# A decoder layer's attention on one core: shorter branch softmax and gate mix on VectorE, one rope product and one shared power on GpSimd, the query scale folded into the keys

## The chip, the cores and the metric

The kernel runs as one program on one core of a Trainium2 chip. Its time is the device time in microseconds (us). A core has TensorE (PE, matrix products), VectorE (DVE), ScalarE (ACT), GpSimd (POOL) and SyncE (SP, which here issues the DMAs). Each engine works through its own list of instructions in order, and the engines wait for one another on semaphores.

## The reference, cut to what matters

The layer is attention, then cross-attention, then a mixture of experts. Only the attention changes. With 64 sequences of 64 tokens, width 128, 8 heads of 64 and one key and value head shared by all heads:

```python
q = rmsnorm(rope(h @ w_qc @ w_qup)); k = rmsnorm(rope(h @ w_k)); v = h @ w_v
scale = 1 / sqrt(64)
kc, vc = means of k and v over blocks of 32 tokens        # two blocks
pc = softmax([q @ kc * scale (masked), sink])             # compressed branch
ps = softmax(q @ k * scale (causal))                      # selected branch
pw = softmax([q @ k * scale (causal, window 64), sink])   # window branch
g = sigmoid(q @ w_gate + b_gate)                          # three gates
gates = g / max(sum(g), 1e-6)
out = (gates[0]*comp + gates[1]*sel + gates[2]*win) @ w_out_group @ w_out
x1 = layernorm(x + out)
```

With only 64 tokens the window covers everything, so the selected and the window branch share one set of exponentials `E` and differ only in their denominators: `Z` (the row's sum) and `Z` plus the sink's exponential.

## The kernel before, in words

The attention works on 32 tiles of 128 rows (two sequences each). Every engine runs through the same list of slots, 41 in all (32 tiles and a lag of 9). In a slot `s` each engine does, for several tiles at once, the stage that tile `s - lag` has reached: a tile has its projection in lag 0, rope and the sums of squares in lag 1 (`b`), the normalised key in lag 2 (`c`), transposes in lag 3 (`d`), scores and exponentials in lag 4 (`e`), the branch denominators and gate mix in lag 5 (`f`), the mixed weights `Pm` on GpSimd in lag 6 (`f` there), the products with `v` in lag 7 (`h`), the output product and the layer norm's statistics in lag 8 (`k`), and the layer norm's output `xo` in lag 9 (`l`). The order of the work inside a slot is written out by hand and is the order in which the engine executes it. Each engine unrolls the list completely, so nothing is reordered at run time.

What the change and the prediction touch, by engine, in the order of a slot:

- VectorE. `xo` of tile `l` (L461, a tensor-scalar operation whose two scalars are read from `mv` and `rs`), the row maxima out of PSUM (L465), the copy `s5` (L468), the negative scaled maximum `nb` (L473), the cosine product `ta` (L478), the block scores `un` (L482), the residual sum `r` (L488), the maximum over the blocks and the sink `mc` (L491, L500), the arguments of the small exponentials (L494, L507, L509), the rope sum (L504, which waits for GpSimd's `tb`), `bn_aggr` (L512), the block means of the keys (L518), the normalised key `kd` (L525), the variance plus epsilon `ve` (L530), the denominators `den` (L533 to L536), the sums of squares (L539), the reciprocals of all six denominators (L542), `ms` (L546), and then the gate mix (L549 to L565), which ends in `pa` and `pc`, the factors for GpSimd.
- GpSimd. The two halves of the sine product `tb` (L401, L403), the gate logits `gl` and arguments (L409, L412; they wait for `s5`), `Pm = E * pa` (L417) and `Pm += pc` (L422), then `rs = ve ** -0.5` (L427, waits for L530), `rinv = ms ** -0.5` for nine columns (L431, waits for L546), and `sc8 = rinv / 8` (L433).
- ScalarE. Eight exponentials with `scale=sc8` that also write the row sums `Z` (L350), the small exponentials `ex` (L356), and copies out of PSUM.

In VectorE's list the operation behind the last one of the gate mix (L565) is the next slot's L461:

```python
if l.live:
    l.wait(dve, ln_rstd)
    l.wait_ring(dve, stored, 16, back=2)
    V.tensor_scalar(xo[:, l.u2, :], r[:, l.u2, :], mv[:, l.u2, 0:1], rs[:, l.u2, 0:1], ...)
```

`ln_rstd` of tile `l` is counted up by L427 in the slot before, while L546 and L431 of that slot come later.

Of the kernel before, what the change touches and what calls it, by code (L numbers as in the profile page):

```python
# [93 lines left out]
def attention(nc, x, xT, table, table64, table32, v_dram, x1, tiles, later, disp):  # L94
# [8 lines left out]
    with ExitStack() as ctx:  # L103
# [22 lines left out]
        root = sb("root", [P, H])  # L126
# [8 lines left out]
        ms = sb("ms", [P, 2, 9])  # L135
        rinv = sb("rinv", [P, 4, 9])
# [32 lines left out]
        ve = sb("ve", [P, 2, 1])  # L169
        rs = sb("rs", [P, 2, 1])  # L170
# [153 lines left out]
        def _(act):  # L324
# [48 lines left out]
        def _(pool):  # L373
# [63 lines left out]
        def _(dve):  # L437
# [18 lines left out]
            def slot(at):  # L456
                b, c, d, e, f, k, l = (Tile(at, m) for m in (1, 2, 3, 4, 5, 8, 9))
                if l.live:
                    l.wait(dve, ln_rstd)
# [80 lines left out]
                if f.live:  # L540
                    n.upto(n_den)
                    n_rd = n.add(V.reciprocal(rd[:, :, :], den[:, :, :]))  # L542
                if b.live:
                    n.upto(n_ss)
                    b.free(dve, inv_rms, 2)
                    V.tensor_scalar(ms[:, b.u2, :], ss[:, :], 1.0 / D, 1e-6, ALU.mult, ALU.add).then_inc(mean_sq, 1)  # L546
                if f.live:
                    n.upto(n_rd)
                    n_gs = n.add(V.tensor_reduce(gs[:, :], rd[:, :, 3:6], AX.X, ALU.add))  # L549
                    n.add(V.tensor_tensor(a1[:, :], rd[:, :, 4], rd[:, :, 0], ALU.mult))  # L550
                    n_a2 = n.add(V.tensor_tensor(a2[:, :], rd[:, :, 5], rd[:, :, 1], ALU.mult))
                    n.upto(n_gs)
                    n_gs = n.add(V.tensor_scalar(gs[:, :], gs[:, :], 1e-6, None, ALU.max))
                    n.add(V.tensor_tensor(a3[:, :], rd[:, :, 2], rd[:, :, 3], ALU.mult))
                    n.upto(n_a2)
                    n.add(V.tensor_tensor(a1[:, :], a1[:, :], a2[:, :], ALU.add))
                    n.upto(n_gs)
                    n_rg = n.add(V.reciprocal(rg[:, :], gs[:, :]))
                if f.live:
                    n.upto(n_rg)  # L560
# [1021 lines left out]
```

## Time and profile before

| | |
|---|---|
| time, median of 3 runs | 776.14 us (773.79 to 778.46) |
| the profiled execution | 769.72 us |
| its span in the trace | 767.9 us |
| busy share of the span: PE, DVE, ACT, POOL | 74%, 71%, 58%, 60% |
| granted TensorE clock, mean | 0.882 |

The span is divided into 40 slices of 19.2 us; the attention fills slices 1 to 16 or so. In the rows below, times are from the start of the span. A row of a timeline has the start in us, the length in us, the engine, the line, the operation, the tensors written and read (`a_` stands for the attention, `x_` for the cross-attention, `m_` for the experts, `l_` for what the later stages share), and their shapes as partitions by columns. In square brackets stands how long the engine was idle before it and what it waited for. An operation's length includes time in which it has started and can't yet read or write; the next one's start can lie before its end.

### The profile page before, as it was taken

Reading aid. Unit: us, or ns where it says so; the run is one execution under the profiler, and the core shown is the slowest. Engines: PE = TensorE matmul, PEld = TensorE weight load, DVE = VectorE, ACT = ScalarE, POOL = GpSimd, SP = SyncE. Lnnn points to the kernel's source line nnn. Section 1 sums busy time; section 2 is a strip of 40 time slices with the busy share of each in tenths; the row PEclk is TensorE's granted clock in tenths of the full one; section 3 lists DMA queues with packets and bytes.
Section 4 is the critical chain, followed back from the end, with each engine's and each line's share of the span. In section 5 each row is a group of like instructions: output and inputs, shape, how many; then the busy total and the mean of one; then the engine's idle time right before and its main releaser. Section 6 shows DMA issues by size and latency. Waiting matters only on the chain. (4 is left out here: it accounts for less than half of the span.)

```text
span 767.9 us, 17025 instructions
## 1 busy us (share of the span) xinstructions
PE 566.4 (74%) x4772; PEld 430.1 (56%) x4772; DVE 547.6 (71%) x1867; ACT 444.8 (58%) x1362; POOL 462.4 (60%) x553
## 2 busy tenths in 40 slices
PE   4766777777767774798999898961004999999984
PEld 2445556555555563465767666651003988888832
DVE  2589999999999985277888878864013666677615
ACT  2588777777777762496787655530002565566506
POOL 4568777777777754465664577787550454555533
PEclk9999889999998889597999998985556999999998
DMA  6154444441111101210111111111111222222154
GB/s 232 35 180 159 168 167 144 165 136 33 34 42 35 37 25 30 76 29 22 43 39 37 33 54 32 33 50 46 38 42 38 55 72 65 67 68 69 41 211 125
DMA packets 65884, 57.78 MB, mean 75 GB/s; under 512 B 22133, under 2 KB 60154, under 8 KB 63490
## 3 DMA queue, kind: packets, MB, share of 16 engines
q1 hardware_dynamic: 60866, 46.14, 19.3%
q0 software_dynamic: 4352, 8.47, 3.3%
q10 hardware_dynamic: 576, 2.10, 0.7%
q8 instruction: 42, 0.69, 0.4%
q14 instruction: 48, 0.39, 0.2%
HBM read 25.86 MB, written 31.33 MB: 74 GB/s over the span
## 5 line engine op out<-in xcount | busy, mean ns | idle before, releaser
L1419 POOL DMA_INDIRECT y_dram<-m_y,m_blk x72 | 72.0, 1000 | 92.1 <-ACT m_y L1385 80.6
L350 ACT ACTIVATE a_E<-a_ps,a_nb,a_sc 128x64 f32<-128x64 f32 x256 | 99.5, 408 | 11.7 <-DVE a_nb L473 10.6
L986 POOL DMA_INDIRECT disp_dram<-l_R,x_pos x64 | 63.0, 984 | 24.8 <-issue 15.1
L431 POOL TENSOR_TENSOR a_rinv<-a_ms,a_halfneg 128x9 f32<-128x9 f32 x32 | 57.7, 1803 | 33.5 <-DVE a_ms L546 33.5
L309 PE MATMUL a_ps<-a_tab,a_xTt 128*128 128x512 f32 x64 | 38.7, 689 | 48.0 <-DVE a_r L488 41.7
L959 POOL TENSOR_TENSOR x_KB<-x_kT,l_table 128x1024 f32<-128x1024 f32 x32 | 61.9, 1935 | 6.9 <-ACT x_kT L907 6.6
L966 POOL TENSOR_TENSOR l_rs<-x_ve,l_halfneg 128x2 f32<-128x2 f32 x32 | 23.9, 748 | 55.6 <-DVE x_ve L1121 55.3
L1289 PE MATMUL m_ps<-l_table,m_blk 128*128 128x128 f32 x72 | 14.6, 285 | 55.9 <-DMA m_blk<-disp_dram 55.9
L1452 DVE TENSOR_SCALAR m_lin<-m_ps 128x512 f32<-128x512 f32 x36 | 24.9, 691 | 41.1 <-PE m_ps L1314 41.1
L350 ACT ACTIVATION_READ_ACCUMULATOR a_E<-a_ps,a_nb,a_sc 128x1 f32 x256 | 53.5, 209 | 0.0
L1367 ACT ACTIVATE m_th<-m_tTc 128x256 fp32r<-128x256 f32 x36 | 15.1, 418 | 61.9 <-DVE m_tTc L1441 61.9
L1075 DVE TENSOR_REDUCE x_mx<-x_ps 128x16 f32<-128x1024 f32 x32 | 39.0, 1218 | 6.6 <-PE x_ps L793 6.3
L317 PE MATMUL a_ps<-a_PT,a_VB 128*128 128x256 f32 x128 | 42.8, 468 | 0.0
L1377 ACT ACTIVATE m_sg<-m_ps 128x512 f32<-128x512 f32 x36 | 21.5, 597 | 35.0 <-PE m_ps L1314 35.0
L279 PE MATMUL a_ps<-a_KB,a_qT 128*64 128x138 f32 x512 | 41.1, 307 | 0.0
L266 PE MATMUL a_ps<-a_tab,a_Pm 128*128 128x128 f32 x128 | 26.4, 342 | 19.3 <-POOL a_Pm L422 19.3
L427 POOL TENSOR_TENSOR a_rs<-a_ve,a_halfneg 128x1 f32<-128x1 f32 x32 | 19.5, 610 | 34.2 <-DVE a_ve L530 34.2
L309 PEld LDWEIGHTS a_ps<-a_tab,a_xTt 128*128 128x128 f32 x64 | 10.4, 204 | 53.1 <-issue 48.1
L793 PE MATMUL x_ps<-x_KB,x_qT 64*64 64x512 f32 x256 | 36.9, 648 | 3.6 <-DVE x_sh L1097 2.8
L1289 PEld LDWEIGHTS m_ps<-l_table,m_blk 128*128 128x128 f32 x72 | 7.6, 145 | 56.4 <-DMA m_blk<-disp_dram 56.4
L892 ACT ACTIVATE x_PT<-x_ps 128x1024 f32<-128x1024 f32 x32 | 32.5, 1015 | 11.4 <-PE x_ps L782 11.3
L422 POOL TENSOR_TENSOR a_Pm<-a_Pm,a_pc 128x512 f32<-128x512 f32 x32 | 37.5, 1173 | 2.5
(234 smaller groups left out, 1990.8 us busy)
## 6 DMA issues: line engine op xcount, KB each, us to landing
disp_dram<-l_R SPq DMA_DIRECT2D x16, 1040.0 KB, 4.2
m_blk<-disp_dram SPq DMA_DIRECT2D x72, 65.0 KB, 1.9
a_xTt<-in_xT SPq DMA_DIRECT2D x32, 64.0 KB, 3.8
l_W1l<-in_w SPq DMA_DIRECT2D x1, 2048.0 KB
a_VB<-v_dram SPq DMA_DIRECT2D x128, 16.0 KB, 2.0
a_xt<-in_x SPq DMA_DIRECT2D x32, 64.0 KB, 2.0
x_dram<-a_xo SPq DMA_DIRECT2D x32, 64.0 KB, 1.7
x_xa<-x_dram SPq DMA_DIRECT2D x32, 64.0 KB, 1.9
```

What stands on the lines that cost most here:

```text
L279: last = nc.tensor.matmul(ps_S[D * q:D * q + D, c // 2, (c % 2) * 2 * W:(c % 2 + 1) * 2 * W], qT[:, e.u2, c, D * q:D * q + D], KB[:, e.u2, ...
L309: nc.tensor.matmul(flat[:, 0:512], xTt[:, a.u2, :], wqkv[:, 0:512], start=True, stop=True)
L317: last = nc.tensor.matmul(ps_mT.rearrange("p (c t) -> p c t", c=4)[:, :, D * q:D * q + D], VB[:, h.u4, q, :], PT[:, :, D * q:D * q + D], s ...
L350: last = nc.scalar.activation(E[:, e.u4, g, :], ps_Sh[:, g // 4, g % 4, 0:D], ACT.Exp, bias=nb[:, e.u2, g:g + 1], scale=sc8[:, e.u4, g:g + 1],
L422: G.tensor_tensor(Pv, Pv, pc[:, f.u2, :, :].rearrange("p h n -> p (h n)").unsqueeze(2) .to_broadcast([P, 2 * H, 32]), ALU.add).then_inc(mi ...
L431: G.tensor_tensor(rinv[:, b.u4, :], ms[:, b.u2, :], halfneg[:, 0:9], ALU.pow).then_inc(inv_rms, 1)
L793: last = nc.tensor.matmul(ps_S[T * q:T * q + T, 8 * g:8 * g + 8, :].rearrange("p h k -> p (h k)"), qT[s, d.t % 6, T * q:T * q + T], KB[s, ...
L892: nc.scalar.activation(PT[:, :, :], ps_PT, ACT.Copy).then_inc(PT_ready, 1)
L959: G.tensor_tensor(KB[:, c.t % 3, :, :, :], kT[:, c.u4, :].rearrange("p (b k) -> p b k", b=2).unsqueeze(2).to_broadcast([P, 2, 8, T]), hm[: ...
L986: G.indirect_dma_start(out=disp[:, :], out_offset=bass.IndirectOffsetOnAxis(ap=pos[:, B % 2, k_, t - base:t - base + 1], axis=0), in_=R[:, ...
L1075: n_mx = n.add(V.tensor_reduce(mx[:, :], ps_S, AX.X, ALU.max))
L1419: G_.indirect_dma_start(out=Y[:, :], out_offset=bass.IndirectOffsetOnAxis(ap=blk[:, (2 * q + j) % NB, P:P + 1].bitcast(I32), axis=0), in_= ...
```

## The change

On VectorE, 35 operations of a full slot become 28. The sink's column is kept in a third column of `un` (now `u3`), so one reduction gives `mc` and one subtraction the three arguments. The row sums go straight into `den`; the gate denominators `dg` stand apart. The weight of a branch is computed as the reciprocal of a product, `wt = 1 / (den * dg * max(gs, 1e-6))`. The factor 1/8 moves from `sc8` into the key's factors `gg`. On GpSimd the two sine products are one operation over 288 columns that reads the halves in swapped order, `sc8` is gone, and while tiles of both kinds are live, `ve` is the tenth column of `ms`, so that one power of ten columns gives `rinv` and the layer norm's `rs`. `xo` (L461's) then waits for that power.

```diff
+        def rstd(t):
+            if t + 7 < tiles:
+                return rinv[:, (t + 7) % 4, 9:10], inv_rms, t + 8
+            return rs[:, t % 2:t % 2 + 1], ln_rstd, t + 8 - tiles
...
# ScalarE
+                    e.free(act, mixing, 2)
...
-                                                    bias=nb[:, e.u2, g:g + 1], scale=sc8[:, e.u4, g:g + 1],
-                                                    accum_out=Z[:, e.u2, g:g + 1])
+                                                    bias=nb[:, e.u2, g:g + 1], scale=rinv[:, e.u4, g:g + 1],
+                                                    accum_out=den[:, e.u2, g, 1:2])
...
# GpSimd
-                    G.tensor_tensor(tb[:, :, 0:16], q[:, :, 16:32],
-                                    sin[:, 0:16].unsqueeze(1).to_broadcast([P, 9, 16]), ALU.mult)
-                    G.tensor_tensor(tb[:, :, 16:32], q[:, :, 0:16],
-                                    sin[:, 16:32].unsqueeze(1).to_broadcast([P, 9, 16]),
+                    G.tensor_tensor(tb[:, :, :].rearrange("p h (w k) -> p h w k", w=2),
+                                    q[:, :, 0:32].rearrange("p h (w k) -> p h w k", w=2)[:, :, ::-1, :],
+                                    sin[:, :].rearrange("p (w k) -> p w k", w=2).unsqueeze(1).to_broadcast([P, 9, 2, 16]),
                                     ALU.mult).then_inc(sined, 1)
...
                 if k.live:
                     k.wait(pool, ln_var)
-                    G.tensor_tensor(rs[:, k.u2, :], ve[:, k.u2, :], halfneg[:, 0:1], ALU.pow).then_inc(ln_rstd, 1)
+                if k.live and not b.live:
+                    G.tensor_tensor(rs[:, k.u2:k.u2 + 1], ve[:, :], halfneg[:, 0:1], ALU.pow).then_inc(ln_rstd, 1)
                 if b.live:
                     b.wait(pool, mean_sq)
                     b.free(pool, exped, 4)
-                    G.tensor_tensor(rinv[:, b.u4, :], ms[:, b.u2, :], halfneg[:, 0:9], ALU.pow).then_inc(inv_rms, 1)
-                    b.wait(pool, inv_rms)
-                    G.tensor_tensor(sc8[:, b.u4, :], rinv[:, b.u4, 0:H], root[:, :], ALU.mult).then_inc(scales, 1)
+                    b.free(pool, x1_done, 11)
+                    w = 10 if k.live else 9
+                    G.tensor_tensor(rinv[:, b.u4, 0:w], ms[:, b.u2, 0:w], halfneg[:, 0:w],
+                                    ALU.pow).then_inc(inv_rms, 1)
...
# VectorE
-                n.add(V.tensor_tensor(gg[:, h, :], gq[:, :], gk[:, :], ALU.mult))
+                n.add(V.scalar_tensor_tensor(gg[:, h, :], gq[:, :], D ** -0.5, gk[:, :], ALU.mult, ALU.mult))
...
                 if l.live:
-                    l.wait(dve, ln_rstd)
+                    inv_std, done, count = rstd(l.t)
+                    dve.wait_ge(done, count)
...
-                    n_mc = n.add(V.tensor_tensor(mc[:, :], un[:, :, 0], un[:, :, 1], ALU.max))
+                    n_mc = n.add(V.tensor_reduce(mc[:, :], u3[:, :, :], AX.X, ALU.max))
...
-                    n_mc = n.add(V.tensor_tensor(mc[:, :], mc[:, :], snk[:, :], ALU.max))
...
-                    n.add(V.tensor_tensor(arg[:, e.u2, :, 0:2], un[:, :, :],
-                                          mc[:, :].unsqueeze(2).to_broadcast([P, H, 2]), ALU.subtract))
-                    n_arg = n.add(V.tensor_tensor(arg[:, e.u2, :, 2], snk[:, :], mc[:, :], ALU.subtract))
+                    n_arg = n.add(V.tensor_tensor(arg[:, e.u2, :, 0:3], u3[:, :, :],
+                                                  mc[:, :].unsqueeze(2).to_broadcast([P, H, 3]), ALU.subtract))
...
-                    V.tensor_scalar(ve[:, k.u2, :], mv[:, k.u2, 1:2], 1e-5, None, ALU.add).then_inc(ln_var, 1)
+                    if b.live and b.t >= 2:
+                        dve.wait_ge(inv_rms, b.t - 1)
+                    if not b.live:
+                        dve.wait_ge(ln_rstd, max(k.t + 7 - tiles, 0))
+                    V.tensor_scalar(ms[:, b.u2, 9:10] if b.live else ve[:, :], mv[:, k.u2, 1:2], 1e-5, None,
+                                    ALU.add).then_inc(ln_var, 1)
...
-                    n.add(V.tensor_reduce(den[:, :, 2], ex[:, f.u2, :, 0:3], AX.X, ALU.add))
-                    n.add(V.tensor_scalar(den[:, :, 3:6], ex[:, f.u2, :, 4:7], 1.0, None, ALU.add))
-                    n.add(V.tensor_copy(den[:, :, 0], Z[:, f.u2, :]))
-                    n_den = n.add(V.tensor_tensor(den[:, :, 1], Z[:, f.u2, :], ex[:, f.u2, :, 3], ALU.add))
+                    n_dg = n.add(V.tensor_scalar(dg[:, :, :], ex[:, f.u2, :, 4:7], 1.0, None, ALU.add))
+                    n.add(V.tensor_reduce(den[:, f.u2, :, 0], ex[:, f.u2, :, 0:3], AX.X, ALU.add))
+                    n_den = n.add(V.tensor_tensor(den[:, f.u2, :, 2], den[:, f.u2, :, 1], ex[:, f.u2, :, 3], ALU.add))
...
-                    n_rd = n.add(V.reciprocal(rd[:, :, :], den[:, :, :]))
+                    n_dd = n.add(V.tensor_tensor(dd[:, :, :], den[:, f.u2, :, :], dg[:, :, :], ALU.mult))
...
# the gate mix: ten operations become six
+                    n_gs = n.add(V.tensor_reduce(gs[:, :], rdg[:, :, :], AX.X, ALU.add))
+                    n.settle()
+                    n.add(V.scalar_tensor_tensor(dd[:, :, :], gs[:, :].unsqueeze(2).to_broadcast([P, H, 3]), 1e-6,
+                                                 dd[:, :, :], ALU.max, ALU.mult))
+                    n.settle()
+                    n.add(V.reciprocal(wt[:, :, :], dd[:, :, :]))
+                    n.settle()
...
```

A reciprocal of `dg` (24 columns) stands ahead of `dd`; `pa` is one addition of two columns of `wt`, and `pc` reads `wt` directly.

## Rows read from the trace of the kernel before

**Rows 1.** The page's head, and VectorE's busy tenths in 40 slices.
```profile
span 767.9 us, 17025 instructions
...
DVE  2589999999999985277888878864013666677615
```

**Rows 2.** Timeline of VectorE over one slot.
```profile
184.98 0.34 DVE L461 TENSOR_SCALAR a_xo<-a_r,a_mv,a_rs 128x128 f32<-128x128 f32 x1
185.24 0.68 DVE L465 TENSOR_REDUCE a_mx<-a_ps 128x8 f32<-128x512 f32 x1
...
186.04 0.76 DVE L478 TENSOR_TENSOR a_ta<-a_qk,a_tab 128x288 f32<-128x288 f32 x1
186.72 0.47 DVE L482 SCALAR_TENSOR_TENSOR a_un<-a_s,a_sc 128x16 f32<-128x16 f32 x1
187.11 0.28 DVE L488 TENSOR_TENSOR a_r<-a_ps,a_xt 128x128 f32<-128x128 f32 x1
...
187.67 1.01 DVE L500 TENSOR_TENSOR a_mc<-a_mc,a_tab 128x8 f32<-128x8 f32 x1
188.60 0.45 DVE L504 TENSOR_TENSOR a_qk<-a_ta,a_tb 128x288 f32<-128x288 f32 x1
188.97 1.02 DVE L507 TENSOR_TENSOR a_arg<-a_un,a_mc 128x16 f32<-128x16 f32 x1
190.81 0.15 DVE L530 TENSOR_SCALAR a_ve<-a_mv 128x1 f32<-128x1 f32 x1
...
192.25 0.10 DVE L546 TENSOR_SCALAR a_ms<-a_ss 128x9 f32<-128x9 f32 x1
...
193.49 0.34 DVE L461 TENSOR_SCALAR a_xo<-a_r,a_mv,a_rs 128x128 f32<-128x128 f32 x1
```

**Rows 3.** Timeline of GpSimd in the same slot.
```profile
188.73 1.22 POOL L422 TENSOR_TENSOR a_Pm<-a_Pm,a_pc 128x512 f32<-128x512 f32 x1
191.03 0.61 POOL L427 TENSOR_TENSOR a_rs<-a_ve,a_halfneg 128x1 f32<-128x1 f32 x1 [1.08 <-DVE a_ve L530]
192.43 1.80 POOL L431 TENSOR_TENSOR a_rinv<-a_ms,a_halfneg 128x9 f32<-128x9 f32 x1 [0.78 <-DVE a_ms L546]
```

**Rows 4.** Timeline of VectorE: `xo` in slot 9 and in slot 33.
```profile
65.41 0.34 DVE L461 TENSOR_SCALAR a_xo<-a_r,a_mv,a_rs 128x128 f32<-128x128 f32 x1
...
270.09 0.34 DVE L461 TENSOR_SCALAR a_xo<-a_r,a_mv,a_rs 128x128 f32<-128x128 f32 x1
```

**Rows 5.** Groups of GpSimd by line and shape: count, busy us, mean ns, idle before.
```profile
L401 POOL TENSOR_TENSOR a_tb<-a_qk,a_tab 128x144 f32<-128x144 f32 x32 | 16.8, 526 | 8.2 <-ACT a_qk L360 8.2
L971 POOL TENSOR_TENSOR x_xr<-x_xb,x_bob 128x128 f32<-128x128 f32 x32 | 14.4, 450 | 0.0
...
L1428 POOL TENSOR_TENSOR m_rs<-m_ve,l_halfneg 128x4 f32<-128x4 f32 x8 | 8.1, 1011 | 17.3 <-DVE m_ve L1487 16.1 <-ACT m_xo L1407 1.2
```

**Rows 6.** Cross-attention: L1028 by source (min/median/max ns), two of it and GpSimd beside.
```profile
L1028 DVE TENSOR_SCALAR l_R<-x_r,x_mv,l_rs x32: 414/546/1989, 349.0 to 521.9; 128x256 f32<-128x256 f32 x32
...
349.02 1.99 DVE L1028 TENSOR_SCALAR l_R<-x_r,x_mv,l_rs 128x256 f32<-128x256 f32 x1
364.27 0.54 DVE L1028 TENSOR_SCALAR l_R<-x_r,x_mv,l_rs 128x256 f32<-128x256 f32 x1 [0.82 <-POOL l_rs L966]
...
348.78 2.08 POOL L959 TENSOR_TENSOR x_KB<-x_kT,l_table 128x1024 f32<-128x1024 f32 x1
364.21 0.45 POOL L971 TENSOR_TENSOR x_xr<-x_xb,x_bob 128x128 f32<-128x128 f32 x1
```

**Rows 7.** Timeline of slot 6, where GpSimd waits for `s5`: VectorE, then GpSimd.
```profile
42.90 0.69 DVE L465 TENSOR_REDUCE a_mx<-a_ps 128x8 f32<-128x512 f32 x1 [1.24 <-PE a_ps L279]
...
45.83 1.02 DVE L507 TENSOR_TENSOR a_arg<-a_un,a_mc 128x16 f32<-128x16 f32 x1
...
44.55 1.05 POOL L417 TENSOR_TENSOR a_Pm<-a_E,a_pa 128x512 f32<-128x512 f32 x1
```

**Rows 8.** Timeline of VectorE in slot 3: the rope sum waits for the sine product.
```profile
25.65 0.46 DVE L504 TENSOR_TENSOR a_qk<-a_ta,a_tb 128x288 f32<-128x288 f32 x1 [1.72 <-POOL a_tb L403]
```

More of the change, by code:

```diff
@@ L125, in attention @@
         halfneg = sb("halfneg", [P, 16])
-        root = sb("root", [P, H])
         xTt = sb("xTt", [P, 2, P])
@@ L134, in attention @@
         ss = sb("ss", [P, 9])
-        ms = sb("ms", [P, 2, 9])
-        rinv = sb("rinv", [P, 4, 9])
+        ms = sb("ms", [P, 2, 10])
+        rinv = sb("rinv", [P, 4, 10])
         kd = sb("kd", [P, 2, 2, D])
@@ L143, in attention @@
         s5 = sb("s5", [P, 2, H, 5])
-        sc8 = sb("sc8", [P, 4, H])
         gl = sb("gl", [P, H, 3])
         nbg = sb("nbg", [P, 3])
-        Z = sb("Z", [P, 2, H])
-        a3 = sb("a3", [P, H])
         nb = sb("nb", [P, 2, H])
-        un = sb("un", [P, H, 2])
+        u3 = sb("u3", [P, H, 3])
         mc = sb("mc", [P, H])
@@ L153, in attention @@
         ex = sb("ex", [P, 2, H, 7])
-        den = sb("den", [P, H, 6])
-        rd = sb("rd", [P, H, 6])
+        den = sb("den", [P, 2, H, 3])
+        dg = sb("dg", [P, H, 3])
+        rdg = sb("rdg", [P, H, 3])
+        dd = sb("dd", [P, H, 3])
         gs = sb("gs", [P, H])
-        rg = sb("rg", [P, H])
-        a1 = sb("a1", [P, H])
-        a2 = sb("a2", [P, H])
+        wt = sb("wt", [P, H, 3])
         pa = sb("pa", [P, 2, H])
@@ L168, in attention @@
         mv = sb("mv", [P, 2, 2])
-        ve = sb("ve", [P, 2, 1])
-        rs = sb("rs", [P, 2, 1])
+        ve = sb("ve", [P, 1])
+        rs = sb("rs", [P, 2])
         xo = sb("xo", [P, 2, P])
@@ L187, in attention @@
         v_spread, v_kept = ([sem(f"{k}{i}") for i in range(4)] for k in ("v_spread", "v_kept"))
-        sined, scores_kept, gate_args, scales = sem("sined"), sem("scores_kept"), sem("gate_args"), sem("scales")
+        sined, scores_kept, gate_args = sem("sined"), sem("scores_kept"), sem("gate_args")
         projected, kq_copied, squared, v_copied = sem("projected"), sem("kq_copied"), sem("squared"), sem("v_copied")
@@ L376, in _ @@
             n.add(G.memset(halfneg[:, :], -0.5))
-            n.add(G.memset(root[:, :], D ** -0.5))
             G.memset(later.blank, 0.0).then_inc(later.pattern_made, 1)
@@ L444, in _ @@
             n.add(V.tensor_copy(maskb[:, :], maskf[:, :]))
+            n.add(V.tensor_copy(u3[:, :, 2], snk[:, :]))
             for h in range(2):
-                n.add(V.tensor_tensor(gg[:, h, :], gq[:, :], gk[:, :], ALU.mult))
+                n.add(V.scalar_tensor_tensor(gg[:, h, :], gq[:, :], D ** -0.5, gk[:, :], ALU.mult, ALU.mult))
             n.add(V.tensor_scalar(wg[:, :], wgate[:, :], gqc[:, 0:1], None, ALU.mult))
@@ L458, in slot @@
                 if l.live:
-                    l.wait(dve, ln_rstd)
+                    inv_std, done, count = rstd(l.t)
+                    dve.wait_ge(done, count)
                     l.wait_ring(dve, stored, 16, back=2)
-                    V.tensor_scalar(xo[:, l.u2, :], r[:, l.u2, :], mv[:, l.u2, 0:1], rs[:, l.u2, 0:1],
+                    V.tensor_scalar(xo[:, l.u2, :], r[:, l.u2, :], mv[:, l.u2, 0:1], inv_std,
                                     ALU.subtract, ALU.mult).then_inc(x1_done, 1)
@@ L470, in slot @@
                     n.upto(n_max)
-                    e.wait(dve, scales)
+                    e.wait(dve, inv_rms)
                     e.free(dve, exped, 2)
-                    V.scalar_tensor_tensor(nb[:, e.u2, :], mx[:, :], -1.0, sc8[:, e.u4, :], ALU.mult,
+                    V.scalar_tensor_tensor(nb[:, e.u2, :], mx[:, :], -1.0, rinv[:, e.u4, 0:H], ALU.mult,
                                            ALU.mult).then_inc(maxed, 1)
@@ L482, in slot @@
                     n_un = n.add(V.scalar_tensor_tensor(
-                        un[:, :, :], s5[:, e.u2, :, 0:2], 1.0 / 32,
-                        sc8[:, e.u4, :].unsqueeze(2).to_broadcast([P, H, 2]), ALU.mult, ALU.mult))
+                        u3[:, :, 0:2], s5[:, e.u2, :, 0:2], 1.0 / 32,
+                        rinv[:, e.u4, 0:H].unsqueeze(2).to_broadcast([P, H, 2]), ALU.mult, ALU.mult))
                 if k.live:
@@ L497, in slot @@
                     n_bn = n.add(V.bn_stats(st[:, :], r[:, k.u2, :]))
-                if e.live:
-                    n.upto(n_mc)
-                    n_mc = n.add(V.tensor_tensor(mc[:, :], mc[:, :], snk[:, :], ALU.max))
                 if b.live:
@@ L540, in slot @@
                 if f.live:
+                    n.upto(n_dg)
+                    n_rdg = n.add(V.reciprocal(rdg[:, :, :], dg[:, :, :]))
                     n.upto(n_den)
-                    n_rd = n.add(V.reciprocal(rd[:, :, :], den[:, :, :]))
+                    n_dd = n.add(V.tensor_tensor(dd[:, :, :], den[:, f.u2, :, :], dg[:, :, :], ALU.mult))
                 if b.live:
@@ L545, in slot @@
                     b.free(dve, inv_rms, 2)
-                    V.tensor_scalar(ms[:, b.u2, :], ss[:, :], 1.0 / D, 1e-6, ALU.mult, ALU.add).then_inc(mean_sq, 1)
+                    V.tensor_scalar(ms[:, b.u2, 0:9], ss[:, :], 1.0 / D, 1e-6, ALU.mult, ALU.add).then_inc(mean_sq, 1)
                 if f.live:
[L548 to L560, printed above, removed]
+                    n.upto(n_rdg)
+                    n_gs = n.add(V.tensor_reduce(gs[:, :], rdg[:, :, :], AX.X, ALU.add))
[5 more added lines that the diff above has]
+                    n.settle()
                     f.free(dve, mixed, 2)
-                    n.add(V.tensor_tensor(pa[:, f.u2, :], a1[:, :], rg[:, :], ALU.mult))
-                    n.add(V.tensor_tensor(a3[:, :], a3[:, :], rg[:, :], ALU.mult))
-                    n.settle()
+                    n.add(V.tensor_tensor(pa[:, f.u2, :], wt[:, :, 1], wt[:, :, 2], ALU.add))
                     V.scalar_tensor_tensor(pc[:, f.u2, :, :], ex[:, f.u2, :, 0:2], 1.0 / 32,
-                                           a3[:, :].unsqueeze(2).to_broadcast([P, H, 2]),
+                                           wt[:, :, 0:1].to_broadcast([P, H, 2]),
                                            ALU.mult, ALU.mult).then_inc(mixing, 1)
```

## The prediction

> **What bounds the kernel now.** I read the page's slices first, then the timeline of VectorE over a slot, then GpSimd's over the same slot. The slices [rows 1] show VectorE at nine tenths or more from slice 4 to slice 14, which is the attention; the later stages are not touched. In the timeline [rows 2] one slot runs from one L461 to the next, 8.51 us, and there is no idle time in brackets in it. From slot 9 to slot 33 it is 24 slots in 204.7 us, 8.53 us each [rows 4]. So each 0.1 us on VectorE's chain is worth 2.4 us in these slots.
>
> VectorE is not at work all of that time. A small operation takes about 0.16 us (L530, 0.15), yet L500 and L507, with 8 and 16 columns, take 1.01 and 1.02, and L482 0.47; L478 takes 0.76 where L504, just as wide, takes 0.45 [rows 2]. L507 starts while GpSimd's L422 runs and ends just as that ends (188.73 + 1.22 = 189.95, against 189.99) [rows 2, 3]. A VectorE operation with two inputs in SBUF stands while a GpSimd operation reads there, and the other way round (L422 takes 1.22, its sibling L417 1.05 [rows 3, 7]). The waits of a slot are 0.31 + 0.31 + 0.85 + 0.86 = 2.3 us; 6.2 us are work. The power L431 does not do this: the small operations between L546 and L461, ten of them behind L546, run beside it in 1.24 us, 0.11 apart [rows 2, 3].
>
> GpSimd is idle for 1.08 + 0.78 = 1.9 us of the slot [rows 3]. What matters is where its power lies: L431 starts 0.18 after L546 and ends at 194.23, 0.74 us after the next L461 has started [rows 2, 3]. Now nobody waits for it in that slot. L461 waits for L427, which ended at 191.64.
>
> **The change, part by part.** VectorE has seven operations fewer. At 0.11 each that is 0.8 us; three new waits on the operation just issued, in the gate mix, take back about 0.1 each (an estimate, two thirds of a small operation's length). I take 0.5 us a slot. Bounds: 0.2 (the waits cost a full 0.2 each) and 0.8. This counts only where VectorE's own list is the bound.
>
> The Trainium skill, page "VectorE: DVE Perf Modes", section "The DRAIN you can't avoid", says that the next operation does not start until the one before has emptied the pipeline. By that rule seven operations would be worth their full 0.16, 1.1 us a slot, and the six slots that gain below would give 3.8 us more. The trace disagrees for small ones: they start 0.11 apart [rows 2]. I go by the rows.
>
> The new wait is the main part. `xo`, first in VectorE's slot, now waits for the ten-column power, which waits for L546. Behind L546 VectorE has only six operations, about 1.05 us by the spacing above with the three waits. The power of ten columns: nine take 1.80 [rows 3], four take 1.01 [rows 5], 0.158 a column, so 1.96 (bounds: 1.80, a free tenth column, and 2.0). From L546's start to L461's start it is then 0.18 + 1.96 + 0.04 = 2.18 us, so VectorE stands for 1.1 us in each slot where both kinds of tile live. Everything in VectorE's list stands behind it: the maxima, and through them the exponentials; ScalarE and TensorE have slack here (VectorE never waits for either in [rows 2]), so they are late without deciding.
>
> Dropping L427 (0.61), `sc8` (0.2) and one of the two sine products shortens GpSimd, but it was idle there, so by itself that gives nothing in these slots. One sine product of 288 columns: 128 columns take 0.45 and 512 take 1.05 [rows 5, 7], which gives 0.70; L401's short rows of 16 cost 0.05 more than that line [rows 5], so I take 0.73. Bounds: 0.70, and 1.05 for two times L401.
>
> The skill's page "GPSIMD Engine Reference", section 3.1, gives 4497 ns for 2048 columns, 2.2 ns a column; an estimate from that is 0.81 us, which would make the sum 1.9 us larger. The rows up to 512 columns show 1.6 ns a column [rows 5, 7], and I keep 0.73.
>
> Now the chain of a slot, with zero at the power's end.
>
> 1. GpSimd goes straight on to the sine product, and VectorE to L461, 0.04 later. L1028 is L461's sibling (a tensor-scalar operation with two scalars out of SBUF) and stands in the same place behind a power. It takes 0.41 us at the least, 1.99 beside the 1024-column L959 that had started before, and 0.54 beside L971, which starts 0.06 ahead of it [rows 6]. So this form waits for GpSimd's reads too, and GpSimd comes first. L461 was spared so far because the power ran beside it. Now it is held until the sine product ends: the next operation starts at 0.72 instead of 0.04 + 0.26.
> 2. From L465 to L482 it was 1.48 us, of which 0.31 was L478's wait for the sine product, now past. But the gate operations and `Pm` come later as well, since GpSimd must wait for `s5`. Slot 6 shows that case: L417 starts 1.65 after L465, and the operation behind the rope sum starts 2.93 after L465, held by L417 [rows 7]. So the subtraction (L507's place) starts at 0.72 + 2.93 = 3.65.
> 3. From there to L530 it was 1.84 us, with L422's hold in it [rows 2]; less L509, 1.76: at 5.41.
> 4. From L530 to L546 it was 1.44 [rows 2]. The copy L535 goes, `dd` comes (0.1 each), and the reciprocal has 24 columns, not 48, for which I take 0.15 (between 0 and 0.3): 1.29, at 6.70.
> 5. L546 to the power 0.18, the power 1.96: 8.84 us.
>
> So the slot grows from 8.53 to 8.84. As a sum: work -0.5, waits for GpSimd's reads -0.3 (2.3 to 2.0; the sine product now holds one operation instead of two), the stand at L461 +1.1. Over 24 slots it is +7.5 us.
>
> **The ends of the attention gain.** In slots 2 to 4 the loop goes L546, power, `sc8`, sine product, L504, L546, and L504 waits for GpSimd [rows 8]. One sine product instead of two saves 0.22, `sc8` with its wait 0.24: three times 0.46, 1.4 us. In slots 7 and 8, and in slots 33 to 36, VectorE's list or the chain through the gate mix is the bound and there is no shared power to wait for: six times 0.48, 2.9 us. Together -4.3 us, between -2 and -6, since in the last slots VectorE also waits for TensorE.
>
> The sum is +7.5 - 4.3 = +3.2 us. Against the profiled execution that is 769.72 to 772.9; the median of the runs is 6.4 above the profiled one, so I forecast 776.14 + 3.2 = 779.3 us. The likeliest case's own range: the cheap bounds together (power 1.80, sine 0.70, ends -6) give -3 us, and a sine product of 0.8 with ends of -2 gives +7: 773 to 783. A sine product at its upper bound is a rival below.
>
> **Rivals.**
>
> - L461 is not held, because VectorE gets in first. For: it starts within 0.1 us of the sine product. Against: rows 6, and that GpSimd starts first there. Then L465 starts at 0.30, the slot is 8.42, 24 x -0.11 = -2.6, with the ends -6.9: 769.2 us, faster. It decides once L461 is held less than 0.1 us.
> - The power doesn't make L461 wait, or by much less, because L546 lies early enough. Then VectorE's list is the bound: 5.7 work and 2.3 waits, 8.0 us, -12.7 in all and -17 with the ends: 759 us. Against: 2.18 us stand against 1.05 us of operations. It would need the power at 0.9 us.
> - The sine product over swapped halves takes 1.05 us or more, as much as the two before: +0.32 a slot, +7.7: 787 us, slower. For: 18 short rows, read backwards by halves, of which no row shows the price.
> - The slot falls to a level set by another engine. `nb` and with it ScalarE's exponentials come 0.4 us later after L461 than now, and TensorE's next scores with them. VectorE showed no wait for either in the slot of before, so I give it little: +0.2 a slot, 784 us.
>
> **How the numbers follow.** Chances: the forecast 0.64, L461 not held 0.14, no wait for the power 0.04, slow sine product 0.12, another engine 0.06. A measurement of this kernel can tell 0.5%, 3.9 us, from no change, so the forecast's +3.2 lies just inside. Its own spread puts 0.24 of its 0.64 above +3.9, 0.38 within, 0.02 below. Slower: 0.24 + 0.12 + 0.05 = 0.41. Faster: 0.02 + 0.11 + 0.04 = 0.17. Same: 0.42. The range from 769 to 787 reaches to the first and the third rival and leaves out the second and the tails.
>
> **What the profile will show.** L461's new form waits about 1.1 us for GpSimd's ten-column power in every slot from 9 to 33, is 0.7 us long instead of 0.34, and the sine product is 0.73 us long. VectorE's digit in the middle slices falls from 9 to 8 (1.1 of 8.8 us idle). GpSimd has some 0.8 us of idle time before `gl`. L504's form is held about 0.65 us, L507's 0.85, L482's not at all. The slot is 8.8 us. The prediction is wrong if the slot is below 8.5 or above 9.0, which would be a wait I placed wrongly, or if the ends give nothing.

## The result: 1.0% slower, by a longer steady slot

The changed kernel takes 784.83 us (median of 4 runs, 780.51 to 788.95) against 776.34 us (773.79 to 778.46) for the one before on the same chip: ratio 1.0098, 95% interval 1.0063 to 1.0134, +8.5 us. The forecast was 779.3, within 769 to 787: the time is inside that range, but above the 773 to 783 of the prediction's likeliest case. The profiled executions differ by more, 780.51 against 769.72 us.

The page of the changed kernel, head, busy times and slices; it answers to [rows 1]:

```profile
span 778.7 us, 16767 instructions
...
PE 563.1 (72%) x4772; PEld 426.0 (55%) x4772; DVE 523.5 (67%) x1644; ACT 443.0 (57%) x1362; POOL 438.6 (56%) x463
...
DVE  2668888888888786268788889863005666666615
...
PEclk9979998998888999598999999965557999999998
```

VectorE's nines in the attention are eights: it has less to do and takes longer. The timeline of VectorE over a slot answers to [rows 2]:

```profile
183.09 0.81 DVE L466 TENSOR_SCALAR a_xo<-a_r,a_mv,a_rinv 128x128 f32<-128x128 f32 x1 [1.24 <-POOL a_rinv L435]
183.82 0.68 DVE L470 TENSOR_REDUCE a_mx<-a_ps 128x8 f32<-128x512 f32 x1
...
184.62 0.45 DVE L483 TENSOR_TENSOR a_ta<-a_qk,a_tab 128x288 f32<-128x288 f32 x1
184.99 0.20 DVE L487 SCALAR_TENSOR_TENSOR a_u<-a_s,a_rinv 128x16 f32<-128x16 f32 x1
...
185.68 1.10 DVE L506 TENSOR_TENSOR a_qk<-a_ta,a_tb 128x288 f32<-128x288 f32 x1
186.70 1.03 DVE L509 TENSOR_TENSOR a_arg<-a_u,a_mc 128x24 f32<-128x24 f32 x1
...
188.47 0.15 DVE L535 TENSOR_SCALAR a_ms<-a_mv 128x1 f32<-128x1 f32 x1
...
189.69 0.16 DVE L553 TENSOR_SCALAR a_ms<-a_ss 128x9 f32<-128x9 f32 x1
...
192.03 0.81 DVE L466 TENSOR_SCALAR a_xo<-a_r,a_mv,a_rinv 128x128 f32<-128x128 f32 x1 [1.24 <-POOL a_rinv L435]
```

And GpSimd's, which answers to [rows 3]:

```profile
183.02 0.80 POOL L403 TENSOR_TENSOR a_tb<-a_qk,a_tab 128x288 f32<-128x288 f32 x1
184.69 0.47 POOL L410 TENSOR_TENSOR a_gl<-a_s,a_rinv 128x24 f32<-128x24 f32 x1 [0.87 <-DVE a_s L473]
...
186.55 1.14 POOL L423 TENSOR_TENSOR a_Pm<-a_Pm,a_pc 128x512 f32<-128x512 f32 x1
189.98 2.01 POOL L435 TENSOR_TENSOR a_rinv<-a_ms,a_halfneg 128x10 f32<-128x10 f32 x1 [2.29 <-DVE a_ms L553]
191.97 0.79 POOL L403 TENSOR_TENSOR a_tb<-a_qk,a_tab 128x288 f32<-128x288 f32 x1
```

One slot is 192.03 - 183.09 = 8.94 us. `xo` (L466) waits 1.24 us for the ten-column power, and is then 0.81 long: it starts 0.07 behind the sine product and ends just after it. In this text an operation is *held* when it has started and stands because GpSimd is reading SBUF, so that its row is longer than alone. The rope sum and the arguments of the small exponentials (L506, L509) are held under `Pm`.

The attention ends with the last `xo`: 311.4 us against 303.9, +7.5. From the first `xo` to that of slot 33 it takes 214.6 us against 204.7 [rows 4], +10.0; up to the first one it is 1.5 us later, and behind slot 33 it gains 3.9. The later stages, whose code is the same, are another 3.3 us longer in this pair of executions. The medians differ by 8.5.

### The profile page after: what moved, and what is told of

It is laid out like the page before. It is cut to its first block and busy times, and to the rows that moved or that the text cites. A ratio compares the mean times of both kernels' runs of the same rounds, so it can differ in the third digit from the quotient of the medians.

```text
span 778.7 us, 16767 instructions
## 1 busy us (share of the span) xinstructions
PE 563.1 (72%) x4772; PEld 426.0 (55%) x4772; DVE 523.5 (67%) x1644; ACT 443.0 (57%) x1362; POOL 438.6 (56%) x463
## 5 line engine op out<-in xcount | busy, mean ns | idle before, releaser
L353 ACT ACTIVATE a_E<-a_ps,a_nb,a_rinv 128x64 f32<-128x64 f32 x256 | 99.6, 408 | 34.8 <-DVE a_nb L478 34.5
L435 POOL TENSOR_TENSOR a_rinv<-a_ms,a_halfneg 128x10 f32<-128x10 f32 (+1 forms) x32 | 62.8, 1963 | 70.6 <-DVE a_ms L553 61.1
L311 PE MATMUL a_ps<-a_tab,a_xTt 128*128 128x512 f32 x64 | 47.9, 839 | 59.0 <-DVE a_r L493 53.3
L353 ACT ACTIVATION_READ_ACCUMULATOR a_E<-a_ps,a_nb,a_rinv 128x1 f32 x256 | 53.2, 208 | 0.0
L1385 ACT ACTIVATE m_y<-m_ps,m_blk 128x128 f32<-128x128 f32 x72 | 22.6, 364 | 44.2 <-PE m_ps L1333 43.6
L1308 PE MATMUL m_ps<-l_W1h,m_th 128*128 x144 | 33.7, 316 | 13.1 <-issue 10.6
L466 DVE TENSOR_SCALAR a_xo<-a_r,a_mv,a_rinv 128x128 f32<-128x128 f32 x25 | 19.9, 797 | 30.7 <-POOL a_rinv L435 30.7
L319 PE MATMUL a_ps<-a_PT,a_VB 128*128 128x256 f32 x128 | 40.5, 448 | 0.0
L1333 PE MATMUL m_ps<-l_table,m_hT 128*128 x288 | 38.3, 276 | 0.6 <-issue 0.6
L1097 DVE TENSOR_TENSOR x_sh<-x_ps,x_mx 128x1024 f32<-128x1024 f32 x32 | 38.6, 1208 | 0.2
```

Of the source, the lines that this page charges most:

```text
L311: nc.tensor.matmul(flat[:, 0:512], xTt[:, a.u2, :], wqkv[:, 0:512], start=True, stop=True)
L319: last = nc.tensor.matmul(ps_mT.rearrange("p (c t) -> p c t", c=4)[:, :, D * q:D * q + D], VB[:, h.u4, q, :], PT[:, :, D * q:D * q + D], s ...
L435: G.tensor_tensor(rinv[:, b.u4, 0:w], ms[:, b.u2, 0:w], halfneg[:, 0:w], ALU.pow).then_inc(inv_rms, 1)
L1097: V.tensor_tensor(sh[:, d.u2, :, :], ps_S, mx[:, :].unsqueeze(2).to_broadcast([P, H, T]), ALU.subtract).then_inc(shifted, 1)
L1308: nc.tensor.matmul(dst[:, p % 2, j, :], left, right[:, bass.ds(e, 1), half * I:(half + 1) * I].rearrange("p a n -> p (a n)"), start=(i == ...
L1333: last = nc.tensor.matmul(ps_y[:, j, :], hT[:, q % 2, 2 * j + c, :], W2[:, bass.ds(expert[2 * q + j], 1), c, :].rearrange("p a n -> p (a n)"),
```

## The experiments

In every run the slot is the distance of two `xo` in the middle of the attention, and the time is compared with the kernel before on the same chip. All keep the whole computation. "The changed kernel" is the one of the diff above.

| kernel | slot, us | last `xo`, us | ratio (95%) |
|---|---|---|---|
| before | 8.53 | 303.9 | |
| changed | 8.94 | 311.4 | 1.0098 (1.0063 to 1.0134) |
| e1: powers apart | 7.76 | 283.5 | 0.9717 (0.9690 to 0.9745) |
| e2: two sine products | 8.64 | 305.3 | 1.0020 (0.9997 to 1.0043) |
| e3: before, shared power | 8.76 | 309.6 | 1.0112 (1.0090 to 1.0134) |
| e4: `xo` late | 7.19 | 270.7 | 0.9548 (0.9515 to 0.9580) |
| e5: before, one sine product | 8.37 | 298.6 | 0.9929 (0.9901 to 0.9957) |
| e6: mix alone | 7.91 | 287.1 | 0.9778 (0.9737 to 0.9819) |
| e7: work under `Pm` | 7.98 | 287.4 | 0.9808 (0.9780 to 0.9837) |
| e8: `xo` late, powers apart | 7.73 | 282.1 | 0.9715 (0.9683 to 0.9748) |
| e9: `Pm`'s time filled | 7.22, 7.36 in turn | 270.0 | 0.9581 (0.9549 to 0.9614) |
| e10: e8, 10 columns | 7.75 | 283.2 | 0.9736 (0.9696 to 0.9776) |
| e11: e4 again | 7.19 | 267.2 | 0.9578 (0.9545 to 0.9611) |
| e12: e8, 11 columns | 7.24 | 268.1 | 0.9567 (0.9537 to 0.9598) |

**e1, the two powers apart again.** The rest of the change stays.

```diff
-G.tensor_tensor(rinv[:, b.u4, 0:w], ms[:, b.u2, 0:w], ..., ALU.pow)          # w = 10
+G.tensor_tensor(rs[:, k.u2:k.u2 + 1], ve[:, k.u2:k.u2 + 1], ..., ALU.pow)
+G.tensor_tensor(rinv[:, b.u4, 0:9], ms[:, b.u2, 0:9], ..., ALU.pow)
```

> The changed kernel with the shared power undone: the layer norm's power is again an operation of its own, early in the slot, and the rope sine product, the gate mix and the scale stay as changed. Theory (the wait of xo for the ten-column power is what costs): xo no longer waits, a slot falls from 8.94 us to about 7.85, and the time is 0.97 to 0.98 of the kernel before. Rival (the rewritten gate mix or the single sine product cost the time themselves): the slot stays above 8.5 us and the time at or above that of before.

The slot is 7.76 us and the kernel 2.8% faster than before. So the shared power alone turns a gain of 0.77 us a slot into a loss of 0.41. What it takes away again is one hold: with the power apart the sine product falls on the cosine product, which then takes 1.06 us, not the 0.45 of L483 in the changed kernel. VectorE, then GpSimd:

```profile
175.95 1.06 DVE L480 TENSOR_TENSOR a_ta<-a_qk,a_tab 128x288 f32<-128x288 f32 x1
```

```profile
175.87 0.82 POOL L401 TENSOR_TENSOR a_tb<-a_qk,a_tab 128x288 f32<-128x288 f32 x1
```

**e2, the changed kernel with two sine products.**

> The changed kernel with the sine product again in two halves. Theory (xo, once released, is held by GpSimd's sine product, 0.80 us long): the first half is about 0.5 us long, xo is held 0.3 us less (0.5 us long, not 0.81), the slot falls from 8.94 to about 8.65, and the time is 7 us below the changed kernel, 1.00 of the kernel before. Rival (VectorE's operation does not wait for GpSimd's reads, or the sine product as a whole sets the slot): the slot stays at 8.94 or grows by the second product's 0.2 us.

`xo` is held for the first half only and is 0.52 long, 0.29 less; the slot, 8.64, is shorter by 0.30:

```profile
178.18 0.52 DVE L467 TENSOR_SCALAR a_xo<-a_r,a_mv,a_rinv 128x128 f32<-128x128 f32 x1 [1.24 <-POOL a_rinv L436]
```

**e3, the kernel before with the shared power and nothing else.**

> The kernel before with the shared ten-column power and nothing else. Theory: xo waits about 1.0 us for the power, the early sine products hold it little because the query scale's operation lies between, the slot is about 8.8 us against 8.53, and the time 1.007 to 1.010 of the kernel before. Rival (the shared power is hidden, since GpSimd has 0.6 us less to do): 8.5 us and 1.000.

Slot 8.76, +0.23. `sc8` lies here between the power and the sine product, so `xo` waits but isn't held, and the sine halves now pass beside the row maxima and not beside the cosine product, which takes 0.45 in place of 0.76 [rows 2]:

```profile
181.78 0.45 DVE L489 TENSOR_TENSOR a_ta<-a_qk,a_tab 128x288 f32<-128x288 f32 x1
...
189.43 0.34 DVE L472 TENSOR_SCALAR a_xo<-a_r,a_mv,a_rinv 128x128 f32<-128x128 f32 x1 [0.93 <-POOL a_rinv L440]
```

**e4, the changed kernel with `xo` behind `r` in VectorE's list**, and e11, the same kernel once more, because e4's profiled execution was its longest (750.91 us).

```diff
-if l.live: ... V.tensor_scalar(xo, ...)       # ahead of mx
 ...
 V.tensor_tensor(r[:, k.u2, :], ps_y, xt[:, k.u2, :], ALU.add)
+if l.live: ... V.tensor_scalar(xo, ...)
```

> The changed kernel with xo moved behind the residual sum r in VectorE's slot, everything else as changed. Theory: the power is done by then, no operation waits for it, the slot is about 8.1 us (the sine product now falls on the block scores and holds them), and the time 0.985 of the kernel before. Rival (the power's end binds through another path, GpSimd's own order): the slot stays at 8.9 us.

> The version with xo late once more, unchanged, so that the two others are compared on one chip: a slot of 7.2 us and 0.955 to 0.96 of the kernel before.

The wait for the power is gone, but the slot is 7.19, 0.9 less than expected. The block scores (L481 here) were to be held by the sine product and aren't: they start 0.08 us ahead of it, and only `xo` behind them is held. VectorE, then GpSimd, in e11:

```profile
151.42 0.17 DVE L481 SCALAR_TENSOR_TENSOR a_u<-a_s,a_rinv 128x16 f32<-128x16 f32 x1
...
151.81 0.56 DVE L492 TENSOR_SCALAR a_xo<-a_r,a_mv,a_rinv 128x128 f32<-128x128 f32 x1
```

```profile
151.50 0.79 POOL L403 TENSOR_TENSOR a_tb<-a_qk,a_tab 128x288 f32<-128x288 f32 x1
```

Whether this order of two starts makes the difference is what e8, e10 and e12 ask.

**e5, the kernel before with one sine product; e6, the kernel before with the new softmax and gate mix** (two sine products, two powers).

> The kernel before with the single sine product of 288 columns and nothing else. Theory: GpSimd has idle time in the slot, and the 0.3 + 0.3 us that the two products held the cosine product and the block scores become one hold of about 0.6 us; the slot stays at 8.5 us and the time at 1.000 of the kernel before, within 0.3%. Rival (fewer GpSimd operations mean less holding): 8.3 us and 0.994.

> The kernel before with the shorter gate mix, branch softmax and folded scale only: two sine products, two powers. Theory: VectorE's list is the bound and is seven operations shorter; with the single sine product the slot was 7.76 us, and the sine product is neutral, so 7.7 to 7.8 us and 0.972 of the kernel before. Rival (the gain seen with the powers apart came from the single sine product as much): about 8.1 us and 0.985.

Slots 8.37 and 7.91: -0.16 and -0.62. Together they make e1, -0.77. For e5 that is its rival, not its theory: the one sine product is worth something by itself. e6 came out between its theory and its rival.

**e7, `xo` late, and the sums of squares, key means and `dg` moved under `Pm`**, `ms` earlier.

> The changed kernel with xo behind r, and with VectorE's operations that read one SBUF or PSUM input (sums of squares, key means, the branch sum, the gate reciprocal) put where GpSimd computes Pm, and those with two SBUF inputs outside it where the data allow. Theory (a hold, not the work, is what remains): the 1.5 us of holds of the version with xo late shrink to 0.5 or less, and ScalarE, with 6.6 us of work a slot, becomes the bound at 6.7 to 6.9 us; 0.94 to 0.945 of the kernel before. Rival (the holds are no queueing but slower operations, which move with them): 7.2 us as with xo late, 0.955.

A miss: 7.98, above the rival's 7.2 too. With `ms` earlier the sine product comes earlier, 0.66 us behind the start of the row maxima and not 1.25 as in e11, and other operations are caught; the sums of squares and the key means come 0.3 us and more behind `Pm`'s end, not under it. VectorE, then GpSimd:

```profile
144.88 0.76 DVE L472 SCALAR_TENSOR_TENSOR a_nb<-a_mx,a_rinv 128x8 f32<-128x8 f32 x1
...
147.63 1.01 DVE L505 TENSOR_SCALAR a_dg<-a_ex 128x24 f32<-128x24 f32 x1
```

```profile
144.82 0.80 POOL L403 TENSOR_TENSOR a_tb<-a_qk,a_tab 128x288 f32<-128x288 f32 x1
...
147.56 1.04 POOL L423 TENSOR_TENSOR a_Pm<-a_Pm,a_pc 128x512 f32<-128x512 f32 x1
```

`nb` has 8 columns and takes 0.76 us, and ScalarE's exponentials wait for it.

**e8, `xo` late with the powers apart.**

> xo behind r as in the version with xo late, but with the layer norm's power as an operation of its own. It asks whether sharing the power is worth anything once nobody waits for it. Theory: GpSimd is idle for 1.6 us before the big power, so the separate one is hidden there; the slot stays at 7.2 us and the time at 0.955 of the kernel before. Rival (GpSimd's length matters now): the slot is 0.3 to 0.6 us longer, 0.965 to 0.975.

Slot 7.73, as the rival said: it loses 0.54 to e4, although both wait for nothing at `xo`. The power has nine columns here, and the sine product starts 0.19 us ahead of the block scores (151.35 against 151.54), which take 0.77.

**e9, e4 with only the part behind the rope sum reordered.**

> The version with xo late, and of VectorE's order only the part behind the rope sum changed: the sums of squares and the key means come while GpSimd makes the first half of Pm, then the subtraction for the exponentials; ms stays just ahead of the gate mix, so that the sine product starts 1.25 us into the slot as there. The version that filled the same gap but moved ms ahead got a slot of 7.98 us, because the sine product then started 0.7 us into the slot and held nb. Theory (where in the slot GpSimd's reads fall is what counts): 6.5 to 6.9 us a slot, ScalarE's 6.6 us of work or TensorE becoming the bound, and 0.94 to 0.945 of the kernel before. Rival (holds only move): 7.2 us or more.

A miss: a slot of 7.29 us on average, some 0.4 above the theory's 6.5 to 6.9 and no better than e4. The sums of squares pass under `Pm` unheld, but in every other slot VectorE waits for TensorE's scores, and `nb` is held again. VectorE, then GpSimd:

```profile
152.99 0.74 DVE L509 TENSOR_REDUCE a_ss<-a_sq 128x9 f32<-128x576 f32 x1
...
157.22 0.69 DVE L464 TENSOR_REDUCE a_mx<-a_ps 128x8 f32<-128x512 f32 x1 [0.69 <-PE a_ps L281]
...
157.95 0.58 DVE L472 SCALAR_TENSOR_TENSOR a_nb<-a_mx,a_rinv 128x8 f32<-128x8 f32 x1
```

```profile
152.71 1.25 POOL L418 TENSOR_TENSOR a_Pm<-a_E,a_pa 128x512 f32<-128x512 f32 x1
...
157.70 0.80 POOL L403 TENSOR_TENSOR a_tb<-a_qk,a_tab 128x288 f32<-128x288 f32 x1
```

So near this slot length VectorE begins to wait for TensorE; whether TensorE sets the slot there was not tested.

**e10, e8 with one useless column in the power (10); e12, with two (11).**

```diff
-w = 9
+w = 11        # e10: 10; ms and rinv wider, ms set to 1.0 once
```

> xo late and the powers apart, as before with a slot of 7.73 us, but the big power takes ten columns, the tenth being a constant that nobody reads: pure extra work of 0.2 us on GpSimd. Theory (phase): the slot with the shared power is shorter (7.19) only because its power ends 0.2 us later, so that the sine product starts at 1.25 us instead of 0.98 and misses the block scores; then this extra work shortens the slot to about 7.2 us, 0.955 of the kernel before. Rival (the shared power saves what GpSimd's separate power of 0.6 us costs): 7.7 to 7.9 us, 0.972 or more.

> The kernel with `xo` late and separate powers, with two useless columns in the normalisation's power (11 instead of 9), nothing else. With 9 and 10 columns the slot was 7.73 and 7.75 us, with `xo` late and the shared power 7.19. Theory (it is when the sine product starts that decides: with the shared power it started 0.08 us behind the block scores' copy and held only `xo`; with 10 columns 0.04 us ahead of it and held it for 0.79): 11 columns make the power 2.16 us, the sine product starts some 0.2 us later, behind the block scores' copy, which then takes 0.2, and the slot falls to 7.2 us although GpSimd does more work; the kernel at 0.957 to 0.965 of the one before. Rival (it is something else in the shared power, such as the one-column power's place in GpSimd's list, that made the slot 7.19): the sine product starts earlier or later with VectorE's list alike, the slot stays at 7.8 us and the kernel at 0.975.

e10 went against the theory (its numbers are the rival's), and e12 shows why. VectorE and GpSimd in e10:

```profile
151.90 0.79 DVE L479 SCALAR_TENSOR_TENSOR a_u<-a_s,a_rinv 128x16 f32<-128x16 f32 x1
...
153.43 1.12 DVE L504 TENSOR_TENSOR a_qk<-a_ta,a_tb 128x288 f32<-128x288 f32 x1
```

```profile
149.94 1.96 POOL L432 TENSOR_TENSOR a_rinv<-a_ms,a_halfneg 128x10 f32<-128x10 f32 x1 [0.64 <-DVE a_ms L547]
151.86 0.80 POOL L401 TENSOR_TENSOR a_tb<-a_qk,a_tab 128x288 f32<-128x288 f32 x1
...
153.20 1.04 POOL L416 TENSOR_TENSOR a_Pm<-a_E,a_pa 128x512 f32<-128x512 f32 x1
```

and in e12:

```profile
149.69 0.45 DVE L475 TENSOR_TENSOR a_ta<-a_qk,a_tab 128x288 f32<-128x288 f32 x1
150.06 0.17 DVE L479 SCALAR_TENSOR_TENSOR a_u<-a_s,a_rinv 128x16 f32<-128x16 f32 x1
...
150.45 0.62 DVE L490 TENSOR_SCALAR a_xo<-a_r,a_mv,a_rs 128x128 f32<-128x128 f32 x1
...
151.35 0.44 DVE L504 TENSOR_TENSOR a_qk<-a_ta,a_tb 128x288 f32<-128x288 f32 x1
```

```profile
148.10 2.12 POOL L432 TENSOR_TENSOR a_rinv<-a_ms,a_halfneg 128x11 f32<-128x11 f32 x1 [0.64 <-DVE a_ms L547]
150.19 0.80 POOL L401 TENSOR_TENSOR a_tb<-a_qk,a_tab 128x288 f32<-128x288 f32 x1
...
151.44 1.25 POOL L416 TENSOR_TENSOR a_Pm<-a_E,a_pa 128x512 f32<-128x512 f32 x1
```

In e10 the sine product starts 0.04 us ahead of the block scores (L479), which stand for it with all of VectorE's list behind them, and then the rope sum (L504) starts 0.23 behind `Pm` and stands under it. In e12 the sine product starts 0.13 behind the block scores. They pass in 0.17, and only `xo` is held by it, 0.62 in place of 0.33. VectorE reaches the rope sum 0.4 us earlier against GpSimd's list, 0.09 ahead of `Pm`, so it takes 0.44. Over the four kernels with `xo` late, the sine product starts 0.19 and 0.04 ahead of the block scores in e8 and e10, and 0.08 and 0.13 behind them in e11 and e12; the slots are 7.73 and 7.75, then 7.19 and 7.24. One more useless column on GpSimd takes the slot from 7.75 to 7.24 us and the kernel from 0.9736 to 0.9567 of the one before.

## Why the prediction was right, and where its terms were off

The mechanism of the steady slot came true with its three terms: by the same count as the prediction's sum, the work fell by 0.48 us a slot (forecast 0.5), the holds from 2.33 to 1.98 (forecast 2.0), and the wait at `xo` is 1.24 (forecast 1.1). The time came out less well. The median moved by 8.5 us where 3.2 were forecast, and 784.83 us lies above the likeliest case's own 773 to 783. The wider range, to 787, holds it only because it was drawn out for a slow sine product, which did not happen: that much is luck. The prediction also left open which way the kernel would go: it gave 0.41 to a loss beyond its mark of 3.9 us, which this is, and 0.42 to no change.

**The new wait at `xo` (the prediction's stand): right.** It is there in 25 slots, 1.24 us long (forecast 1.1). e1 without it is 1.18 us a slot shorter and e3 with it alone 0.23 longer: in e3 the wait is 0.93 and takes 0.8 us of holds away with it (the cosine product, the block scores and `mc`), while the changed kernel waits 1.24, its shorter list being done sooner, has `xo` held for another 0.47, and is rid of only the 0.61 at the cosine product. Behind `ms` VectorE has five operations, where the prediction says six; their 1.10 us is near its 1.05.

**`xo` held by the sine product: right in place and nearly in size.** From the power's end to the next operation it is 192.76 - 191.99 = 0.77 us (forecast 0.72). `xo` itself is 0.52 and 0.34 long in e2 and e3, where half a sine product or the 8-column `sc8` follows the power at once. The sine product takes 0.80 us, not the 0.73 that the prediction kept; its other estimate, 0.81, holds a fixed part that its working doesn't show, since its 2.2 ns a column give 0.63 for 288 columns. The Trainium skill, page "SBUF — State Buffer", section "Who interferes with whom", says that VectorE and GpSimd share a pair of SBUF ports, which the one that issues first has for its whole instruction while the other blocks; that a VectorE operation with two inputs in SBUF contends with a GpSimd operation that reads SBUF, and a tensor-scalar operation can when it runs in a two-port mode; and that a tensor reduction never does. These rows agree: L466 stands for L403, e7's 24-column L505 for L423, while e9's reduction L509, out of SBUF, takes 0.74 in the midst of `Pm`, as long as alone (0.75). Which mode L466 and L505 run in no row shows.

**The slot: 8.94, forecast 8.84.** By the chain's five steps: 0.77 (0.72), then L470 to L509 2.88 (2.93), L509 to L535 1.77 (1.76), L535 to L553 1.22 (1.29), L553 to the power's end 0.29 + 2.01 = 2.30 (2.14). The last is the mis-sized term: `ms` takes 0.16, not the 0.10 of [rows 2], the power starts 0.29 behind it and not 0.18, and its ten columns take 2.01 and not 1.96. Over 24 slots +10.0 in place of +7.5.

**"The ends of the attention gain", 4.3 us: they gain 2.4.** Two errors and a gain:

- Slot 8 was counted among the slots that gain 0.48. It has the ten-column power already, and slot 9's `xo` waits for it. In the changed kernel the last rows before the first `xo` are

```profile
58.37 0.69 DVE L470 TENSOR_REDUCE a_mx<-a_ps 128x8 f32<-128x512 f32 x1 [0.78 <-PE a_ps L281]
...
66.88 0.81 DVE L466 TENSOR_SCALAR a_xo<-a_r,a_mv,a_rinv 128x128 f32<-128x128 f32 x1 [1.13 <-POOL a_rinv L435]
```

  8.51 us from maxima to `xo`, before it was 7.40 (58.01 to 65.41): +1.1 where -0.5 stood.
- The first slots gained about what was said, 0.95 us at the first maxima (27.17 against 28.12), and lost it in slots 5 to 7. There VectorE waits 3.06 us for scores that take 2.11 us in place of 1.16:

```profile
41.03 2.11 PE L281 MATMUL a_ps<-a_KB,a_qT 128*64 128x138 f32 x16
```

```profile
43.19 0.69 DVE L470 TENSOR_REDUCE a_mx<-a_ps 128x8 f32<-128x512 f32 x1 [3.06 <-PE a_ps L281]
```

  The granted clock in the window from 40 to 45 us was 0.50 here, the 1.2 GHz level, and 1.00 before, the 2.4 GHz level. The windows of the changed kernel, with the clock as the third number from the end:

```profile
35.00:40.00 5.00, 2.11 (x9) 1.44 (x9) 4.72 (x23) 3.89 (x18) 1.45 (x3) 0.84 0.65 238
40.00:45.00 5.00, 4.52 (x24) 3.28 (x25) 1.90 (x10) 2.24 (x8) 2.73 (x5) 0.50 0.09 20
```

  TensorE had waited 3.37 us for ScalarE just before, here and, as long, in the kernel before, whose scores then took 1.16. TensorE here, then before:

```profile
40.48 0.62 PE L277 MATMUL a_ps<-a_maskb,a_idb 128*128 128x276 bf16 x2 [3.37 <-ACT a_E L353]
```

```profile
41.37 0.40 PE L275 MATMUL a_ps<-a_maskb,a_idb 128*128 128x276 bf16 x2 [3.37 <-ACT a_E L350]
41.69 1.16 PE L279 MATMUL a_ps<-a_KB,a_qT 128*64 128x138 f32 x16
```

  So that wait alone doesn't tell the two apart. Whether the change brings the lower clock about isn't settled: from 42 to 46 us e3 shows 0.50 too, the other kernels of the experiments 0.57 to 0.86, and there is one profile of each.
- The last slots gained 3.9 us, where four times 0.48 stood. 1.8 of it is in slot 33 and 1.4 in slot 35; their parts were not followed up.

**The rival "the power doesn't make `xo` wait", 759 us,** is what e1 shows without the shared power: 755.51. Its working (8.0 us a slot, VectorE's list the bound: 5.7 of work and 2.3 of holds) was 0.24 too long: in e1 the holds are 0.61 + 0.65 + 0.85 = 2.1 us. The other rivals didn't come up. `xo` was held; the sine product takes 0.80 us, not 1.05 (0.83 in e5); VectorE waits for no engine but GpSimd in a steady slot, and that the rival of another engine was priced at 784 us, near the measured time, is chance.

**Where the expected gain went.** The shorter mix and the one sine product were worth 0.77 us a slot (e1), 2.8% of the kernel. The shared power used it up. It saved GpSimd an instruction of 0.6 us, time that it had no use for, and tied `xo`, first in VectorE's list, to the last operation of GpSimd's. With `xo` six operations later in the list, behind `r`, the same change is 4.2 to 4.5% faster than the kernel before (e4, e11), and e12 reaches the same with the powers apart.

What stays open: why the ends gained as they did, the 3.3 us of the unchanged stages, and whether a phase better than that of e4 and e12 is there; e7 and e9, made to find one, didn't. That the order of the two starts sets the slot is shown by e12 against e10, where one useless column is all that differs; for e4 against e8 it is read from the same rows.

## What to carry to other kernels

Sharing an operation saves its fixed cost, and everything that reads one of its results now waits for the last of all its inputs: look at what stands first in the list of the engine that reads it, and move that reader behind work that doesn't need it. Where two engines shut each other out, the slot depends on which of two operations starts first, so cost a reorder by laying both timelines over each other and not by adding lengths. A few columns of useless work, or one operation moved, is a cheap way to test that phase.

## What the runs showed of the hardware

- More work on GpSimd can make the kernel faster: 9, 10 and 11 columns in the power (1.80, 1.96, 2.12 us) give slots of 7.73, 7.75 and 7.24 us. In e10 two starts 0.04 us apart decide over 0.6 us of VectorE's time: the block scores take 0.79 there and 0.17 in e12.
- GpSimd's power doesn't shut VectorE out, though it reads SBUF: in e12 the cosine product L475, 288 columns with two inputs in SBUF, starts at 149.69 in the midst of the power (148.10 to 150.22) and takes 0.45 us, its free length. By the Trainium skill's page named above, "SBUF — State Buffer", section "Who interferes with whom", it would wait; the measurement decides.
- GpSimd's power costs 0.16 us a column from 9 to 11 columns (1.80, 1.96, 2.12), and a single column takes 0.59 us (e1) to 0.61 (before).
- In the attention, time taken off VectorE's steady chain comes out of the kernel to 85% or more: from before to e12 the last `xo` moved by 35.8 us and the median by 34.1, to e11 by 36.7 and 32.5, to e10 by 20.7 and 17.7.
